# A 4-layer decoder: in its two 32-channel cross-attentions, GpSimd adds the key halves ahead of the product with ones, the maxima are split in four steps, and the inverse moves between the maxima

## The reference, cut to what matters

```python
def _L0_xattn_ref(q, k, v):            # q = layernorm(x); k = v = ctx; all 4 x 256 x 256
    N_HEAD = 8
    qh = q.reshape(b * h, d // h, m)   # 32 rows of one head, 256 columns
    kh = k.reshape(b * h, d // h, -1)
    vh = v.reshape(b * h, c // h, -1)
    scale = 1.0 / jnp.sqrt(jnp.asarray(d // h, dtype=q.dtype))
    qk = jnp.einsum('bdm,bdn->bmn', qh, kh) * scale
    sm = jax.nn.softmax(qk, axis=-1)
    ret = jnp.einsum('bmn,bcn->bcm', sm, vh)
    return ret.reshape(b, c, m)
# layer 1: the same, and the result is multiplied by one number, gamma
x = x + _L0_xattn_ref(_layernorm(x, axis=-1), ctx_2048, ctx_2048)
...
x = x + _L1_xattn_ref(_layernorm(x, axis=-1), ctx_2048, ctx_2048, L1_xattn_gamma)
```

## Time and profile before

| | |
|---|---|
| Time, median of 3 runs (range) | 1229.24 us (1228.14 to 1231.35) |
| Profiled execution, its own time | 1234.22 us |
| Its span, first to last instruction | 1232.5 us |
| Busy share of the span: PE, DVE, ACT, POOL | 88%, 63%, 47%, 32% |
| Cross-attention of layer 0 | 164.7 to 219.9 us of the span |
| Cross-attention of layer 1 | 368.0 to 421.7 us of the span |

### The profile page before, as it was taken

How to read it: one execution, slowest core, us unless ns; L and a number is a source line. 1 busy time by engine, 2 the same in 40 slices (tenths; PEclk the granted TensorE clock), 3 DMA queues, 4 the chain that set the end, 5 groups by cost and what they waited for, 6 DMA issues and landing times. The chain is left out here.

```text
span 1232.5 us, 22607 instructions
## 1 busy us (share of the span) xinstructions
PE 1079.9 (88%) x8219; PEld 663.6 (54%) x8234; DVE 772.0 (63%) x2293; ACT 573.6 (47%) x1193; POOL 389.8 (32%) x500
## 2 busy tenths in 40 slices
PE   5778899796999979989888889899999979876898
PEld 2446645365775444445555544457777545552465
DVE  5743366658568534466888578573354576859855
ACT  3758425473344443345555445434533134538443
POOL 2445303200000300013565515516777123852000
PEclk9878899898989989999999899999999999986999
DMA  9100000000004012000000000236666400000001
GB/s 369 44 1 3 1 1 2 1 1 1 1 21 203 2 44 94 0 1 2 2 3 2 2 1 2 108 128 192 191 195 176 137 1 2 2 2 0 1 2 35
DMA packets 23485, 60.73 MB, mean 49 GB/s; under 512 B 3681, under 2 KB 12009, under 8 KB 22480
## 3 DMA queue, kind: packets, MB, share of 16 engines
q1 hardware_dynamic: 18864, 48.92, 11.5%
q0 software_dynamic: 4512, 10.37, 2.7%
HBM read 52.95 MB, written 8.29 MB: 50 GB/s over the span
## 5 line engine op out<-in xcount | busy, mean ns | idle before, releaser
L898 ACT ACTIVATE PT<-PS 128x384 f32<-128x384 f32 (+1 forms) x320 | 153.2, 530 | 168.1 <-PE PS L680 123.7
L269 PE MATMUL PS<-identb 128*128 128x512 bf16 x420 | 105.3, 390 | 7.5 <-PEq L633 3.0
L816 DVE CUSTOM_DVE_ANT_0 junk<-PS,TRI 128x128 bf16<-128x128 f32 (+1 forms) x384 | 110.3, 352 | 0.4 <-PE PS L661 0.4
L661 PE MATMUL PS<-KS,QM 32*128 32x128 f32 (+1 forms) x768 | 86.7, 346 | 22.8 <-ACT PT L898 14.9
L661 PEld LDWEIGHTS PS<-KS,QM 32*128 32x128 f32 x768 | 67.5, 184 | 56.6 <-DVE QM L850 26.5
L680 PE MATMUL PS<-QM,KS 32*128 32x256 f32 (+1 forms) x768 | 89.3, 350 | 1.4 <-ACT PT L898 1.4
L950 POOL TENSOR_SCALAR_AFFINE_SELECT PT<-PT 128x512 f32<-128x512 f32 x96 | 60.4, 636 | 76.3 <-ACT PT L898 76.3
L972 POOL TENSOR_TENSOR OD<-OD 128x256 f32<-128x256 f32 x16 | 11.6, 727 | 229.8 <-DVE OD L870 229.8
L746 PE MATMUL PS<-PT,VM 128*32 128x256 f32 (+1 forms) x1024 | 73.1, 361 | 4.3 <-POOL PT L950 3.7
L1214 POOL TENSOR_TENSOR ROT<-RC,RS 128x512 f32<-128x512 f32 x16 | 20.3, 1269 | 175.8 <-DVE RS L1203 174.5
L269 PEld LDWEIGHTS PS<-identb 128*128 128x128 bf16 x420 | 39.3, 101 | 56.7 <-issue 21.5
(11 more groups left out here) (384 smaller groups left out, 2659.2 us busy)
## 6 DMA issues: line engine op xcount, KB each, us to landing
WD<-w2d_in SPq DMA_DIRECT2D x47, 256.0 KB, 3.2
WU<-w2u_in SPq DMA_DIRECT2D x1, 5632.0 KB, 17.1
WA<-wl_in SPq DMA_DIRECT2D x1, 5137.0 KB, 15.7
GB<-gate_rows SPq DMA_DIRECT2D x8, 512.0 KB, 8.5
WU<-chosen SPq DMA_DIRECT2D x16, 256.0 KB, 5.3
WB<-wb_in SPq DMA_DIRECT2D x1, 3208.0 KB, 18.4
WA<-wa_in SPq DMA_DIRECT2D x1, 2560.0 KB, 16.1
WA<-w2s_in SPq DMA_DIRECT2D x6, 384.0 KB, 16.5
```

What stands on the lines that cost most here:

```text
L269: pe.matmul(PS[:, bank, :].rearrange("p (a n) -> p a n", a=4), identb[:], identb[:].rearrange("p (a n) -> p a n", a=1).to_broadcast([P, 4, ...
L661: return pe.matmul(PS[:, s, m * T:m * T + n], queries(U, v)[rows, m * P:(m + 1) * P], keys(U, v)[rows, 0:n], start=True, stop=True, skip_g ...
L816: last = dve.tensor_tensor_reduce(junk[:, s, m * P:m * T + P], PS[:, s, m * T:m * T + (m + 1) * P], TRI[:, (1 - m) * P:T], 1.0, NEG, ALU.a ...
L898: act.activation(PT[:, g % 3, st_slot(k), 0:W], PS[:, st_bank(g, k), 0:W], ACT.Exp, scale=scale).then_inc(S["at_exp"], 1)
```

## The change

In both cross-attentions with 32 channels, three things differ.

- POOL gets a new step, `paired(g)`: it adds the two key halves of `PT` (columns 0 to 255 and 256 to 511) into a new tile `PAIRED`, two heads at a time, so two instructions of 128 x 512 for a unit. Each waits for two exponentials. The step stands ahead of scaled(g-3) in POOL's loop. PE's product with ones reads `PAIRED`: 4 matmuls in place of 8. PE's order is also turned round: the product with ones (`product_sums`) comes ahead of half 1, and the one with the values (`product_values`) after it.
- `parts` has four steps in place of five. Steps 3 and 4 are `scalar_tensor_tensor`, which compute -m - (first part) and -(rest) - (second part). Steps 2, 3 and 4 read two tiles in SBUF. Step 3 doesn't wait for step 2.
- `invert(g-2)` moves from the end of DVE's iteration to between the two maxima of unit g+2, for g = 2 to 5. The last four inverses stay at the end of their iterations.

```diff
-                            pe.wait_ge(S["at_parts"], d["at_parts"] + 5 * g + 5)
+                            pe.wait_ge(S["at_parts"], d["at_parts"] + 4 * g + 4)
...
+                    def product_sums(g):
+                        pe.wait_ge(S["at_paired"], d["at_paired"] + 2 * g + 2)
+                        if g:
+                            pe.wait_ge(S["at_copied"], d["at_copied"] + g)
+                        for s in range(4):
+                            at = 32 * s
+                            last = pe.matmul(PS[at:at + 32, 7, T:2 * T], ones[:, 0, :], PAIRED[:, s, :], start=True, stop=True,
+                                             skip_group_check=True, tile_position=(0, at))
+                        last.then_inc(S["at_sums"], 1)
+
+                    def product_values(g):
                         for n in range(2):
                             for s in range(4):
                                 at = 32 * s
+                                last = pe.matmul(PS[at:at + 32, 7, 0:T], values(g, n)[:, at:at + 32], PT[:, g % 3, s, n * T:(n + 1) * T],
+                                                 start=False, stop=n == 1, skip_group_check=True, tile_position=(0, at))
+                        last.then_inc(S["at_pv"], 1)
...
-                            (product if r == 1 else product_both)(g - 1, 0)
+                            if r == 1:
+                                product_sums(g - 1)
...
-                            (product if r == 1 else product_both)(g - 1, 1)
+                            if r == 1:
+                                product_values(g - 1)
...
-                        steps = [lambda: dve.tensor_scalar(col(0), M4[:, g % 2], -1.0, None, ALU.mult),
-                                 lambda: dve.tensor_tensor(R4[:, g % 2], M4[:, g % 2], col(0), ALU.add),
-                                 lambda: dve.tensor_scalar(col(1), R4[:, g % 2], -1.0, None, ALU.mult),
-                                 lambda: dve.tensor_tensor(S4[:, g % 2], R4[:, g % 2], col(1), ALU.add),
-                                 lambda: dve.tensor_scalar(col(2), S4[:, g % 2], -1.0, None, ALU.mult)]
                         dve.wait_ge(S["at_max"], d["at_max"] + 2 * g + 2)
+                        m, rest = M4[:, g % 2], R4[:, g % 2]
+                        dve.tensor_scalar(col(0), m, -1.0, None, ALU.mult).then_inc(S["at_parts"], 1)
+                        dve.wait_ge(S["at_parts"], d["at_parts"] + 4 * g + 1)
+                        dve.tensor_tensor(rest, m, col(0), ALU.add).then_inc(S["at_parts"], 1)
+                        dve.scalar_tensor_tensor(col(1), m, -1.0, col(0), ALU.mult, ALU.subtract).then_inc(S["at_parts"], 1)
+                        dve.wait_ge(S["at_parts"], d["at_parts"] + 4 * g + 3)
+                        dve.scalar_tensor_tensor(col(2), rest, -1.0, col(1), ALU.mult, ALU.subtract).then_inc(S["at_parts"], 1)
...
                             maxima(g + 2, 0)
+                            if r == 1 and g >= 2:
+                                invert(g - 2)
                             maxima(g + 2, 1)
...
-                        if g >= 2 and (g - 2) % r == r - 1:
+                        if g >= 2 and (g - 2) % r == r - 1 and (r > 1 or g + 2 >= NQ):
                             invert((g - 2) // r)
...
+                    def paired(g):
+
+                        for half in range(2):
+                            pool.wait_ge(S["at_exp"], d["at_exp"] + 4 * g + 2 * half + 2)
+                            if half == 0 and g:
+                                pool.wait_ge(S["at_sums"], d["at_sums"] + g)
+                            s = st_slot(2 * half)
+                            pool.tensor_tensor(PAIRED[:, s:s + 2, :], PT[:, g % 3, s:s + 2, 0:T], PT[:, g % 3, s:s + 2, T:2 * T],
+                                               ALU.add).then_inc(S["at_paired"], 1)
...
+                        if g < NQ and r == 1:
+                            paired(g)
...
                         if g >= 3 and (g - 3) % r == r - 1:
                             scaled((g - 3) // r)
```

More of the change, by code:

```diff
@@ L606, in shifted_attention @@
             if r == 1:
-                M4, R4, S4 = (tmp(x, [P, 2, 2, 4]) for x in ("MA", "MB", "MC"))
+                M4, R4 = (tmp(x, [P, 2, 2, 4]) for x in ("MA", "MB"))
+                PAIRED = tmp("PAIRED", [P, 4, T])
+                for name, before in (("at_paired", "cap_inv"), ("at_sums", "cap_scaled")):
+                    if name not in S:
+                        S[name] = S[before]
+                        done[name] = done[before]
+                d = dict(done)
                 MR = tmp("MR", [P, 2, T], BF16)
@@ L750, in product_both @@
                             last.then_inc(S["at_pv"], 1)
[L752 to L757, removed]
+                    def product_sums(g):
[8 more added lines that the diff above has]
+                    def product_values(g):
                         for n in range(2):
-                            lo, hi = spans[n]
                             for s in range(4):
                                 at = 32 * s
[L762 to L769, removed]
+                                last = pe.matmul(PS[at:at + 32, 7, 0:T], values(g, n)[:, at:at + 32], PT[:, g % 3, s, n * T:(n + 1) * T],
+                                                 start=False, stop=n == 1, skip_group_check=True, tile_position=(0, at))
+                        last.then_inc(S["at_pv"], 1)
                     if norm is not None:
@@ L781, in _ @@
                         if g >= 1:
-                            (product if r == 1 else product_both)(g - 1, 0)
+                            if r == 1:
+                                product_sums(g - 1)
+                            else:
+                                product_both(g - 1, 0)
                         both(ahead, here, 1)
                         if g >= 1:
-                            (product if r == 1 else product_both)(g - 1, 1)
+                            if r == 1:
+                                product_values(g - 1)
+                            else:
+                                product_both(g - 1, 1)
                         else:
@@ L829, in parts @@
                         col = lambda c: MX[:, g % 2].rearrange("p m (s c) -> p m s c", s=4)[:, :, :, c]
-                        steps = [lambda: dve.tensor_scalar(col(0), M4[:, g % 2], -1.0, None, ALU.mult),
-                                 lambda: dve.tensor_tensor(R4[:, g % 2], M4[:, g % 2], col(0), ALU.add),
-                                 lambda: dve.tensor_scalar(col(1), R4[:, g % 2], -1.0, None, ALU.mult),
-                                 lambda: dve.tensor_tensor(S4[:, g % 2], R4[:, g % 2], col(1), ALU.add),
-                                 lambda: dve.tensor_scalar(col(2), S4[:, g % 2], -1.0, None, ALU.mult)]
-                        dve.wait_ge(S["at_max"], d["at_max"] + 2 * g + 2)
[L836 to L839, removed]
+                        dve.wait_ge(S["at_max"], d["at_max"] + 2 * g + 2)
+                        m, rest = M4[:, g % 2], R4[:, g % 2]
[5 more added lines that the diff above has]
+                        dve.scalar_tensor_tensor(col(2), rest, -1.0, col(1), ALU.mult, ALU.subtract).then_inc(S["at_parts"], 1)
                     def shift(g):
@@ L997, in shifted_attention @@
                             ("at_out", UNITS), ("at_added", 0 if output(0)[1] is False else UNITS),
-                            ("at_parts", 5 * NQ if r == 1 else 0), ("at_flipped", 2 * UNITS), ("at_blank", 1 if r > 1 else 0),
+                            ("at_parts", 4 * NQ if r == 1 else 0), ("at_flipped", 2 * UNITS), ("at_blank", 1 if r > 1 else 0),
                             ("at_sided", 3 * UNITS if r > 1 else 0)):
                 done[name] += k
+            if r == 1:
+                done["at_paired"] += 2 * NQ
+                done["at_sums"] += NQ
     def project(w, nq, hd, QT, KT, V, kernels, arrived, first):
```

## The result

The changed kernel takes 1263.87 us (median of four runs, 1260.16 to 1267.82), the one before 1228.94 (four runs, 1228.14 to 1231.35): 1.0267 times as long, 95% interval 1.0242 to 1.0293. So it is slower by 34.9 us, where 5.8 had been forecast, and outside the range given.

A forecast was written before the change was run, and what follows sets the result against it. PE's own work was taken as the bound (4.80 us a period), with DVE nearly equal. Each stage was to lose 3.05, two stages 6.1, less 0.34: +5.8, so 1235.0 us; 8-in-10 range 1226.8 to 1240.5.

The forecast's parts named there:

- W: Experiments' theory: scaled behind the additions delays ACT's copy to OD, then exponentials and product with ones; not in the forecast.
- P: Experiments' theory: POOL's instructions hold DVE's small steps of parts; the forecast booked such holding.
- The turn at layer 0's start: PE's turn after DVE's first parts in layer 0: starts earlier with four steps, -0.34 us; layer 1: 0.
- the loop of 4.99: Half 1 to half 1, with step 2 of parts held until POOL's addition ends: 4.99 us in place of 4.80.
- steps beside scaled: Parts' steps 3 and 4 on DVE lose to one instruction of scaled: 0.55 us in three units a stage.
- the dear rival: Parts on DVE: step 1 waits too, steps lose to both instructions of scaled; +10.1 us, 1239.3; chance 0.20 including step 1.
- POOL has room: POOL's additions (2.54) and scaled (two of 0.73) fit in 4.80 us; two things follow: a chain of 4.48, held parts.
- the end of the stage: Last period but one 4.48 for about 4.55 (-0.07); last half 1 to first warm matmul 5.35 for 5.03 (+0.32).
- The granted clock stays 1.00 there: PE's clock in both stages keeps its upper level; a fall would cost more than all the rest.
- Not held: Rival: POOL doesn't hold DVE's 128 x 8 steps; -2.1 us, 1227.1; chance 0.16.
- PE's own pace: Rival: both stages run at PE's own work, 0.43 less a unit; -6.9 us, 1222.3; chance 0.05.
- In ahead of scaled: Rival: DVE's small steps wait for the addition but precede scaled on POOL; +2.5 us, 1231.7; chance 0.21.

The follow-up runs named there:

- e7: Changed kernel plus 6 warm matmuls (10 for the last unit) on PE ahead of each product with ones from g = 4; ratio 1.0165 to the kernel before.
- e1: Changed kernel with scaled(g-3) ahead of paired(g) in POOL's loop, nothing else; ratio 1.0110 to the kernel before.
- e4: Kernel before plus POOL's additions behind scaled, read by nobody; ACT waits for them before overwriting PT; ratio 1.0100 to the kernel before.
- e3: Changed kernel without POOL's additions, with the old products; four steps and moved inverse stay; ratio 1.0011 to the kernel before.
- e8: e1 with the second addition of unit g also waiting until parts(g+2) is done; ratio 1.0021 to the kernel before.
- e5: e8 with PE's old order (product with ones last), PAIRED in two buffers, inverse back at the end of DVE's iteration; ratio 0.9955 to the kernel before.
- e6: e5 without the second addition's wait for parts; ratio 1.0029 to the kernel before.
- e10: e4 with each addition replaced by a memset of 128 x 1024, which only writes; ratio 1.0034 to the kernel before.

## Why the prediction was wrong

**Where the 35.4 us are.** Each part is a difference between two kernels: 10.9 is the clock (after less e7), 12.2 is W (e7 less e1), 12.2 is P (e1 less before). But W and P share units, and the parts don't simply add. The seven periods of layer 0 come to 39.7 us in e7 and to the same 39.7 in e1, against 33.1 before: with W's loop of 6.7 gone, the held steps make periods of 6.2 by themselves, and in one unit more (6.21 in e1, 5.25 in e7). All of W's 12.2 stands behind the last turn, where e7 takes 16.44 and 16.88 and e1 10.60 twice. No run takes P away and leaves W, so what P alone is worth in the changed kernel was not measured. Nor are the borders sharp otherwise. e1 itself had clocks of 0.94 and 0.97 in its stages, and e7 adds a few matmuls, so that W may be a little larger and P a little smaller; but e4, at full clock, puts P at 12.4. The forecast had 6.1 in the stages, nearly all of it P.

**Steps that held.** The product with ones: 0.57 and 8 records, as worked out. POOL's addition: mean 1.265 for 1.27. The turn at layer 0's start: 5.93 after the first scores in place of 6.23, -0.30 for -0.34, and 0 in layer 1. The first unit: turn 4.25 after half 1, for 4.21, and then 0.78. Step 2 ends 0.03 after POOL. The first period on the loop of 4.99 is 5.03.

**A term mis-sized: steps beside scaled.** It was put at 0.55 a unit for three units, between bounds of 0 and 1.2, and step 1 at nothing. The row that decided was the reciprocal's 0.20. It was the wrong neighbour: step 1 takes 0.69 beside POOL, while the same reciprocal still takes 0.20. Where W is taken out (e1), the period is the dear rival's 6.19, and the stages lose 12.2, not far from that rival's 10.4. The Trainium skill (VectorE: DVE Perf Modes, section Mode 2×_2P) had said that a tensor_scalar of step 1's form reads through both ports. The traces agree in so far as step 1 is held: 0.69 in the changed kernel and in e1, 0.51 in e3. The range had taken this rival in up to 1240.5; with 12.2 the time would have been 1241.1, so this term alone would have brought it to the edge of the range and a little past it.

**The step that failed: "POOL has room", with "two things follow".** The sum of POOL's work, 4.00 in a period (2.54 and 1.46), does fit. But the prediction asked only who waits for the addition and whom it holds on the port. `scaled(g-3)` was moved in time, by an order of instructions that the diff shows, and nobody who waits for `scaled` was looked up: ACT's copy waits for it through `at_out`, the exponentials stand behind the copy in ACT's queue, and half 1 behind the product with ones. Most of the 6.74 can be worked out from the rows of before: 1.40 + 1.08 + 0.06 + 1.27 + 2 x 0.73 give 5.27 from half 1 to the end of scaled, and ACT's copy and the product with ones (0.57) come on top: at least 5.84. That is above every loop of the prediction, and it would have shown the change as a loss of over 1 us for each unit behind the first scaled.

In the sum, the term that this broke most is the end of the stage, booked at -0.07 and +0.32. The prediction let "four of about 1.5" of scaled run behind the last addition, hidden by the warm matmuls. But `OD` has two buffers, and the last product with ones waits (`at_copied`) for the copy that waits for the first of these four. Layer 0 has 8.30 and 10.00 for the booked 4.48 and 5.35; at full clock (e7) it is 6.71 and 7.57, and with W undone (e1) 4.44 and 5.30.

**A second step that failed: "The granted clock stays 1.00 there".** It went with loops of 4.99 and 5.54, in which PE idles 0.6 to 1.2 a period. With 2.2 in a period the clock fell. (The size of the waits doesn't settle it: e4, with waits of 0.94 to 0.98 a period, stayed at 1.00, and e8 fell once after 0.77.) In the changed kernel these are the windows of layer 0, before, in and after its first fall, and then to the last product:

```profile
165.00:194.90 29.90, 24.01 (x286) 12.24 (x286) 26.19 (x57) 12.91 (x23) 11.53 (x10) 1.00 0.01 2
195.20:198.50 3.30, 3.30 (x30) 1.12 (x22) 2.98 (x8) 1.08 (x2) 1.62 (x2) 0.50 0.00 0
198.80:208.60 9.80, 6.15 (x82) 3.17 (x78) 6.91 (x13) 3.75 (x8) 5.76 (x7) 1.00 0.00 0
208.80:227.10 18.30, 14.90 (x98) 6.58 (x94) 2.65 (x8) 4.62 (x9) 10.72 (x12) 0.50 0.01 2
```

PE had waited 1.76 and then 0.44 us just before the first fall, and 1.00 and 1.24 before the second, which lasts to the end of the loop. 0.50 is the lower of the two levels, 1.2 GHz. Sixteen records of a product cost 1.94 there (L772) in place of 1.07, and the 20 warm matmuls, over which the clock was 0.81 (227.10 to 232.70), 5.54 in place of 4.49. The prediction did say that a fall would cost more than all the rest; it cost 10.9, nearly twice the whole sum of the forecast, which gave it no chance.

**The rivals.** "Not held" and "PE's own pace" are out, since every kernel with both additions and nothing to hold them back shows steps of 0.6 to 1.2. "In ahead of scaled" is out: POOL's next instruction starts as the held step ends, and the next step that it can hold finds it running. "Step 1 waits too, and the steps lose to both instructions of scaled" was right for P.

**The inverse.** It was booked as 0.09 gained against 4.80; by itself it costs +0.27 a unit (e3), through an earlier scaled beside step 1. It was off the path in the kernel before, and e5, which leaves it at the end, is the faster one.

## What to carry to other kernels

When a step is put ahead of another on an in-order queue, list what the later one frees (buffers first) and follow those who wait for it round the loop back to the step itself; an engine's total work tells nothing of this. Tiny DVE steps on the critical path, of the forms that were held here, cost what POOL's instruction beside them has left, so either place POOL's work elsewhere or hold it back with a wait until they are through (e5 against e6: 9.2 us in two stages). And where a loop gives PE waits of a microsecond, the clock must be one of the cases that get a chance.

## What the runs showed of the hardware

- A DVE instruction of 128 x 8 with two inputs in SBUF is held like one of 512 columns: 0.17 becomes up to 1.23 (e4), and in the rows shown it ends 0.03 after POOL's. The Trainium skill (SBUF — State Buffer, section Who interferes with whom) makes no exception for size: by it the order of issue decides who waits, and not the shape.
- When POOL has its next instruction queued, it starts within 0.1 us of a held step's end and gets in ahead of the next dependent step that it can hold; in one unit three of the four steps lose (0.69, 0.63, 0.69).
- POOL's memset of 128 x 1024 (0.97) doesn't hold a two-input step (0.17) but holds the tensor_scalar from f32 to bf16 (0.69). The same section of the Trainium skill has the first, and by its table DVE and GpSimd share a write port too, which would explain the second; e10's rows agree with both.
- Transposes, the reciprocal, the copy from PSUM and the maxima kept their times beside POOL (0.42 to 0.45, 0.20 to 0.21, 0.25 to 0.29, 1.19 to 1.23).
- Whether the clock fell was not the same in like stages: e8 had 1.00 in layer 0 and 0.86 in layer 1 with the same periods. What decides there wasn't settled.
